# Gated cross-attention and FFN on one core: statements of the head and of the tail put in another order

## The reference, cut to what matters

```python
def xattn(query, ctx, mask, Wq, bq, Wk, bk, Wo, bo):        # one head of 256
    Q, K = query @ Wq.T + bq, ctx @ Wk.T + bk
    scores = where(mask[:, None, None, :], -inf, Q K^T)      # 16 batches, 128 x 128 each
    return softmax(scores) @ ctx @ Wo.T + bo                 # V is ctx itself

def ffn(x, weights, scale, bias):
    w = (weights >= 0) * 2 - 1
    return clip((x @ w.T) * scale + bias, -100, 100)

x = x + tanh(g_xattn) * xattn(layernorm(x), ctx, ...)        # x, ctx: 16 x 128 x 256, fp32
x = x + tanh(g_ffn) * ffn(layernorm(x), ...)
```

## Time and profile before

| what | value |
|---|---|
| median of 3 runs | 76.68 us (76.57 to 77.14) |
| the profiled execution's own time | 76.77 us |
| its span (first to last instruction) | 74.9 us |
| TensorE (PE) busy | 68.6 us, 92% |
| VectorE (DVE) busy | 57.9 us, 77% |
| GpSimd (POOL) busy | 53.7 us, 72% |
| ScalarE (ACT) busy | 42.9 us, 57% |
| mean granted TensorE clock | 0.993 |

### The profile page before, as it was taken

The page is one execution under the profiler, slowest core; times in us unless marked ns, Lnnn a source line. Parts: engine busy times, 40 slices in busy tenths (PEclk is TensorE's granted clock), DMA queues, the critical chain, the costliest instruction groups (busy, mean ns, idle before and its releaser), DMA issues.

```text
span 74.9 us, 1593 instructions
## 1 busy us (share of the span) xinstructions
PE 68.6 (92%) x509; PEld 64.2 (86%) x509; DVE 57.9 (77%) x186; ACT 42.9 (57%) x116; POOL 53.7 (72%) x107
## 2 busy tenths in 40 slices
PE   4999988999999999999999999999999999988700
PEld 4988777999999999999999999999999999844400
DVE  0082996975965778999899989999959895949780
ACT  1501528489989639963977495669548607453000
POOL 4000327988989989497999899989899589984700
PEclk9999999999999999999999999999999999999997
DMA  0898999999970000004000300210040000080133
GB/s 6 278 264 214 289 280 244 257 347 371 346 235 30 4 4 4 9 0 140 0 0 27 113 0 9 94 47 0 0 140 1 0 0 0 13 276 4 65 103 113
DMA packets 8229, 8.10 MB, mean 108 GB/s; under 512 B 537, under 2 KB 8093, under 8 KB 8221
## 3 DMA queue, kind: packets, MB, share of 16 engines
q1 hardware_dynamic: 8212, 8.00, 35.1%
q10 hardware_dynamic: 8, 0.00, 0.0%
HBM read 5.90 MB, written 2.10 MB: 107 GB/s over the span
## 4 chain that ended last, share of the span: by engine, by line
PE 75%; DVE 9%; ACT 4%; issue 4%; POOL 3%; POOLq 1%; ACTq 0%
PE ps_K L630 15%; PE ps_Z L630 13%; PE ps_S L630 10%; PE ps_xT L625 8%; PE ps_O L708 8%; PE ps_F L630 8%; PE ps_F L758 6%; PE ps_cT L625 3%; PE ps_S L700 2%; POOL y_biased L371 2%; POOL y_clip L344 1%; DVE y_biased L490 1%; POOLq L41 1%; ACT K_sb L212 1%; DVE out_sb L501 1%
## 5 line engine op out<-in xcount | busy, mean ns | idle before, releaser
L371 POOL TENSOR_TENSOR y_biased<-y_scaled,bias_g 128x256 f32<-128x256 f32 x14 | 11.7, 859 | 2.4 <-DVE y_scaled L510 2.0
L367 POOL TENSOR_TENSOR xb_sb<-x_sb,bo_g 128x256 f32<-128x256 f32 x16 | 11.4, 737 | 0.0
L222 ACT ACTIVATE p_sb<-t_sb,smin 128x128 f32<-128x128 f32 x16 | 6.4, 401 | 8.0 <-DVE smin L453 8.0
L630 PE MATMUL ps_Z<-woT_hi,cT_hi 128*128 128x256 f32 x32 | 9.7, 303 | 0.0
L212 ACT ACTIVATE K_sb<-ps_K,u_col 128x256 f32<-128x256 f32 x14 | 5.9, 474 | 6.5 <-PE ps_K L630 6.5
L630 PE MATMUL ps_K<-cT_hi,wqk_hi 128*128 128x256 f32 x30 | 8.8, 295 | 0.3 <-DVE cT_lo L440 0.3
L630 PE MATMUL ps_Z<-woT_hi,cT_lo 128*128 128x256 f32 x32 | 9.0, 283 | 0.0
L630 PE MATMUL ps_Z<-woT_lo,cT_hi 128*128 128x256 f32 x32 | 9.0, 282 | 0.0
L630 PEld LDWEIGHTS ps_S<-K_sb,xT 128*128 128x128 f32 x64 | 8.2, 191 | 0.8 <-issue 0.4
L630 PE MATMUL ps_S<-K_sb,xT 128*128 128x128 f32 x64 | 8.6, 277 | 0.2 <-ACT K_sb L248 0.2
L630 PE MATMUL ps_K<-cT_lo,wqk_hi 128*128 128x256 f32 x30 | 8.5, 283 | 0.0
(11 more groups left out here) (130 smaller groups left out, 199.7 us busy)
## 6 DMA issues: line engine op xcount, KB each, us to landing
x_sb<-in_x_dram SPq DMA_DIRECT2D x8, 256.0 KB, 7.9
ctx_sb<-in_ctx_dram SPq DMA_DIRECT2D x8, 256.0 KB, 7.7
out_dram<-out_sb SPq DMA_DIRECT2D x7, 256.0 KB, 2.1
wq_sb<-in_L_xattn_Wq_dram SPq DMA_DIRECT2D x1, 256.0 KB, 3.0
wk_sb<-in_L_xattn_Wk_dram SPq DMA_DIRECT2D x1, 256.0 KB, 3.2
wo_sb<-in_L_xattn_Wo_dram SPq DMA_DIRECT2D x1, 256.0 KB, 5.5
mask_u<-in_mask_BxS_bk_dram SPq DMA_DIRECT2D x1, 256.0 KB, 6.2
w_sb<-in_L_ffn_weights_dram SPq DMA_DIRECT2D x1, 256.0 KB, 7.5
```

What stands on the lines that cost most here:

```text
L222: nc.scalar.activation(p_sb[:, g % 2, b], t_sb[:, g % 2, b], ACT.Exp, scale=-1.0, bias=smin[:, r:r + 1], accum_out=psum_p[:, r:r + 1]).the ...
L367: nc.gpsimd.tensor_tensor(xb_sb[:, r], x_sb[:, r], bo_g[:], ALU.add).then_inc(xb_done, 1)
L371: nc.gpsimd.tensor_tensor(y_biased[:, g % 2, b], y_scaled[:, g % 2, b], bias_g[:, 0], ALU.add).then_inc(biased_done, 1)
L630: last = nc.tensor.matmul(dst, lhsT, rhs, start=(n == 0), stop=(n == len(pairs) - 1))
```

## The change

Head: on VectorE `stats_x(0)` and the addition of eps move in front of the first weight split, and the normalising of group 0 in front of the second; `stats_x(1)` goes behind the copy of the transposed x of group 0, `stats_x(2)` behind `split_cT(1)`; `w_mid` moves from ScalarE to VectorE; `stats_x(3)` goes from in front of the loop into round 1, behind `scale_y(0)`. On GpSimd `norm_of_x(3)` goes into round 1, behind `rstd_of_x1(0)` and in front of `add_bo(1)`. On ScalarE `normalise_x(2)` goes behind `evict_K(1)`, and `exp(1, 0)` in front of `evict_xT(2)`. On TensorE `transpose_x(0)` goes in front of `project_first_K(0)`, whose six products now wait one by one for their operands; `scores(0)` becomes `first_scores`, whose first half needs only the first half of K; in round 1 `scores(1)` goes in front of `transpose_x(2)`.

Tail: `add_x1(4)` on VectorE goes behind the row minima, the scaling of group 6 and the last reciprocals. The add of group 6 is split: first batch on GpSimd, second on VectorE, behind `last_y(0)`. Clip and add of the last group's first batch go to GpSimd, behind the two `rstd_of_last_x1`. GpSimd's `clip(6)` waits for `add_x1(4)`, whose buffer it writes. The stores' waits follow.

```diff
@@ sync
-                if g == L - 2:
-                    sp.wait_ge(pool_out_done, GB)
+                if g < L - 2:
+                    sp.wait_ge(out_done, g + 1)
                 else:
-                    sp.wait_ge(out_done, g + 1 if g < L - 2 else g)
+                    sp.wait_ge(pool_out_done, GB + g - L + 2)
+                    if g == L - 1:
+                        sp.wait_ge(out_done, L - 1)
...
@@ scalar
-            normalise_x(2)
             for i in range(1, L):
                 evict_K(i)
                 if i == 1:
-                    act.wait_ge(w_mean_ready, 1)
...
-                evict_xT(i + 1)
-                exp(i, 0)
+                    normalise_x(2)
+                    exp(1, 0)
+                    evict_xT(2)
+                else:
+                    evict_xT(i + 1)
+                    exp(i, 0)
                 evict_x1T_hi(i - 1)
                 exp(i, 1)
@@ gpsimd
             mask_terms(1)
-            norm_of_x(3)
             fold_affine()
...
                 if i == 1:
                     rstd_of_x1(0)
+                    norm_of_x(3)
                     add_bo(1)
...
             add_bias(L - 1)
+            pool.wait_ge(out_done, L - 2)
             clip(L - 1)
+            add_x1_of(L - 1, 0)
             for b in range(GB):
                 rstd_of_last_x1(b)
+            pool.wait_ge(last_biased_done, 1)
+            nc.gpsimd.tensor_scalar(y_clip[:, L % 2, 0], y_biased[:, L % 2, 0], lim[:, 0:1], lim[:, 1:2],
+                                    ALU.min, ALU.max).then_inc(pool_clip_done, 1)
+            add_x1_of(L, 0)
@@ vector
+            stats_x(0)
...
             dve.wait_ge(wqk_hi_ready, 1)
             nc.vector.tensor_tensor(wqk_lo[:, 0], ...)
-            stats_x(0)
...
+            dve.wait_ge(rstd_first_done, 1)
+            ...xn[:, b] of group 0...
             dve.wait_ge(wqk_hi_ready, DC)
             nc.vector.tensor_tensor(wqk_lo[:, 1], ...)
             split_cT(0)
...
-            stats_x(1)
             dve.wait_ge(xT_prod, 1)
             nc.vector.tensor_scalar(xT[:, 0], ps_xT, 1.0, None, ALU.add).then_inc(xT_done, 1)
+            stats_x(1)
...
-            stats_x(2)
             mask_and_min(0)
             split_cT(1)
+            stats_x(2)
...
-            stats_x(3)
+            dve.wait_ge(w_mean_ready, 1)
+            for c in range(DC):
+                nc.vector.tensor_scalar(w_mid[:, c], w_sign2[:, c], w_mean[:, c:c + 1], None, ALU.add).then_inc(w_mid_ready, 1)
             for i in range(1, L):
...
                 scale_y(i - 1)
                 if 2 <= i < L - 1:
                     add_x1(i - 2)
+                if i == 1:
+                    stats_x(3)
                 if i + 3 < G:
                     stats_x(i + 3)
...
-            add_x1(L - 3)
             mask_and_min(L)
...
                 nc.vector.reciprocal(recip_p[:, r:r + 1], psum_p[:, r:r + 1]).then_inc(recip_done, 1)
+            add_x1(L - 3)
...
+            last_y(0)
             dve.wait_ge(pool_clip_done, 2 * GB)
-            nc.vector.tensor_tensor(out_sb[:, rows(L - 1)], y_clip[:, (L - 1) % 2], x1_sb[:, rows(L - 1)], ALU.add
+            nc.vector.tensor_tensor(out_sb[:, L * GB - 1], y_clip[:, (L - 1) % 2, 1], x1_sb[:, L * GB - 1], ALU.add
                                     ).then_inc(out_done, 1)
-            last_y(0)
-            clip_last(0)
             last_y(1)
-            add_last_x1(0)
-            clip_last(1)
-            add_last_x1(1)
+            clip_last_y()                      # clip and add of the second batch
@@ tensor
+            transpose_x(0)
             project_first_K(0)
-            transpose_x(0)
...
-            scores(0)
+            first_scores()                     # chunk c = 0 of both batches waits for K_done 1, c = 1 for K_done 2
...
                 if i == 1:
                     attend(0)
+                    scores(1)
                     transpose_x(2)
+                    transpose_ctx(2)
+                    transpose_x1(0)
+                    pe.wait_ge(w_mid_ready, DC)
+                    transposes(ps_wT, w_mid).then_inc(ps_wT_ready, 1)
                 else:
                     transpose_x(i + 1)
                     attend(i - 1)
-                scores(i)
...
```

More of the change, by code:

```diff
@@ L177, in _ @@
             for g in range(L):
-                if g == L - 2:
-                    sp.wait_ge(pool_out_done, GB)
-                else:
-                    sp.wait_ge(out_done, g + 1 if g < L - 2 else g)
+                if g < L - 2:
+                    sp.wait_ge(out_done, g + 1)
+                else:
+                    sp.wait_ge(pool_out_done, GB + g - L + 2)
+                    if g == L - 1:
+                        sp.wait_ge(out_done, L - 1)
                 sp.dma_start(out_rows[:, rows(g), :], out_sb[:, rows(g), :]).then_inc(stored, 16)
-            for b in range(GB):
-                sp.wait_ge(out_done, L - 1 + b + 1)
-                sp.dma_start(out_rows[:, L * GB + b, :], out_sb[:, L * GB + b, :]).then_inc(stored, 16)
+            sp.wait_ge(pool_out_done, GB + 2)
+            sp.dma_start(out_rows[:, L * GB, :], out_sb[:, L * GB, :]).then_inc(stored, 16)
+            sp.wait_ge(out_done, L)
+            sp.dma_start(out_rows[:, L * GB + 1, :], out_sb[:, L * GB + 1, :]).then_inc(stored, 16)
             sp.wait_ge(stored, 16 * (G + 1))
@@ L345, in clip, with add_x1_of @@
                                             ALU.min, ALU.max).then_inc(pool_clip_done, 1)
+            def add_x1_of(g, b):
+                pool.wait_ge(pool_clip_done, GB * (g - L + 2) + b + 1)
+                nc.gpsimd.tensor_tensor(out_sb[:, GB * g + b], y_clip[:, g % 2, b], x1_sb[:, GB * g + b], ALU.add
+                                        ).then_inc(pool_out_done, 1)
             def add_x1(g):
                 for b in range(GB):
-                    pool.wait_ge(pool_clip_done, b + 1)
-                    nc.gpsimd.tensor_tensor(out_sb[:, GB * g + b], y_clip[:, g % 2, b], x1_sb[:, GB * g + b], ALU.add
-                                            ).then_inc(pool_out_done, 1)
+                    add_x1_of(g, b)
             def scale_weights(c):
@@ L491, in last_y, with clip_last_y @@
                                                in1=bias_g[:, 0], op0=ALU.mult, op1=ALU.add).then_inc(last_biased_done, 1)
-            def clip_last(b):
-                dve.wait_ge(last_biased_done, b + 1)
-                nc.vector.tensor_scalar(y_clip[:, L % 2, b], y_biased[:, L % 2, b], lim[:, 0:1], lim[:, 1:2],
+            def clip_last_y():
+                r = B - 1
+                dve.wait_ge(last_biased_done, GB)
+                nc.vector.tensor_scalar(y_clip[:, L % 2, 1], y_biased[:, L % 2, 1], lim[:, 0:1], lim[:, 1:2],
                                         ALU.min, ALU.max).then_inc(clip_done, 1)
[L498 to L501, removed]
+                dve.wait_ge(clip_done, L - 1)
+                nc.vector.tensor_tensor(out_sb[:, r], y_clip[:, L % 2, 1], x1_sb[:, r], ALU.add).then_inc(out_done, 1)
             def scale_y(g):
@@ L538, in _ @@
                                         ).then_inc(wq_neg_ready, 1)
+            stats_x(0)
+            dve.wait_ge(mv_x_done, GB)
+            nc.vector.tensor_scalar(ve_x[:, rows(0)], mv_x[:, rows(0), 1], EPS, None, ALU.add).then_inc(ve_first_done, 1)
             dve.wait_ge(wqk_hi_ready, 1)
@@ L541, in _ @@
                                     ).then_inc(wqk_lo_ready, 1)
-            stats_x(0)
-            dve.wait_ge(mv_x_done, GB)
-            nc.vector.tensor_scalar(ve_x[:, rows(0)], mv_x[:, rows(0), 1], EPS, None, ALU.add).then_inc(ve_first_done, 1)
+            dve.wait_ge(rstd_first_done, 1)
+            for b in range(GB):
+                nc.vector.tensor_scalar(xn[:, b], x_sb[:, b], mv_x[:, b, 0:1], rstd_x[:, b:b + 1], ALU.subtract, ALU.mult
+                                        ).then_inc(xn_first_done, 1)
             dve.wait_ge(wqk_hi_ready, DC)
@@ L662, in project_first_K @@
             def project_first_K(m):
-                pe.wait_ge(cT_lo_done, 1)
-                pe.wait_ge(wqk_lo_ready, DC)
-                accumulate(ps_K0[m], K_pairs(0, m)).then_inc(ps_K0_ready, 1)
+                w = [[t[:, c, m * P:(m + 1) * P] for c in range(DC)] for t in (wqk_hi, wqk_lo)]
+                pairs = ([(w[0][c], cT_hi[:, 0, c]) for c in range(DC)] + [(w[1][c], cT_hi[:, 0, c]) for c in range(DC)]
+                         + [(w[0][c], cT_lo[:, 0, c]) for c in range(DC)])
+                for n, (lhsT, rhs) in enumerate(pairs):
+                    if n == 0:
+                        pe.wait_ge(wqk_hi_ready, DC)
+                        pe.wait_ge(cT_hi_done, 1)
+                    elif n == DC:
+                        pe.wait_ge(wqk_lo_ready, DC)
+                    elif n == 2 * DC:
+                        pe.wait_ge(cT_lo_done, 1)
+                    last = nc.tensor.matmul(ps_K0[m], lhsT, rhs, start=(n == 0), stop=(n == len(pairs) - 1))
```

(14 more changed lines are left out.)

7 lines of the change are left out of this document (removed).

## The result

The changed kernel takes **82.58 us** (median of 6 runs, 82.17 to 82.91), the kernel before 76.81 beside it (6 runs, 76.57 to 77.35): **1.074 times, interval 1.069 to 1.079, slower by 5.8 us**. The profiled execution took 82.62 with a span of 80.8, against 74.9.

A forecast was written before the change was run, and what follows sets the result against it. TensorE, busy throughout the 48.80 us middle stretch, was taken as the bound. Group 3's chain 4.3, head 0.2 and tail 0.2 sum to 4.7; 76.77 + 4.7 = 81.5, as a median 81.4 us, range 79.9 to 83.2.

The forecast's parts named there:

- the likeliest case: Whole kernel: group 3's chain delays TensorE, head and tail add a little, the clock stays up; 81.4 us, chance 0.58.
- the first rival: Clock falls to the lower level in TensorE's stall in round 1, costing 1.3 us more: 82.7 us, chance 0.28.
- the waits of ScalarE and GpSimd: Sign in the profile after: ScalarE waits for GpSimd's last norm step, GpSimd for VectorE's statistics of group 3.
- the wait for the copy: Sign in round 1: TensorE waits for the copy of x of group 2, before transpose_x1(0).
- the wait before `scores(2)`: Sign behind the stall: TensorE waits before scores(2), forecast to start at 30.7 against 26.45.
- adds of 1.1 in the tail: Sign in the tail: adds of about 1.1 on both VectorE and GpSimd, 0.68 and 0.73 alone.
- Group 3's chain up to its transposes: Round 1, from scale_y(0) over VectorE, GpSimd and ScalarE: TensorE transposes group 3 at about 28.7, not 25.14, +3.5 us.
- `attend(1)`, forecast +3.7: Behind the stall: evict_PT(1), queued behind normalise_x(3), is late, so attend(1) starts at 29.3 against 25.58.
- The step to `scores(2)`: Behind attend(1): scores(2) waits for the copy of group 3's transposed x, +4.3 us in all, bounds 4.0 to 4.6.
- The clock, forecast at nothing in the likeliest case: Around the stall: three stretches of TensorE work speak against a fall; as a rival priced at 1.3, bounds 0.3 and 3.5.
- The head, forecast +0.2: Head to round 1: TensorE's lead of about 0.85 is lost at residual(0) and transpose_x1(0); +0.2, between -0.4 and +0.5.
- The tail, forecast +0.2 within -0.5 to +0.4: Tail: last x1 may come earlier, but VectorE and GpSimd adding at once take longer; +0.2 us.

The follow-up runs named there:

- e3: Changed kernel with fourteen products of zeros on TensorE between K of group 2 and transpose_x(3): 81.05 us, ratio 1.0556 to the kernel before.
- e1: Changed kernel with group 3's statistics and factors back in front of the loop, head and tail still changed: 77.02 us, ratio 1.0009 to the kernel before.
- e2: Kernel before with only group 3's two statements, stats_x(3) and norm_of_x(3), moved into round 1: 82.19 us, ratio 1.0728.
- e4: Changed kernel with only VectorE's stats_x(3) back in front of the loop, norm_of_x(3) left in round 1: 77.11 us, ratio 1.0036 to the kernel before.
- e5: Kernel before with the whole tail of the change and nothing else: 76.66 us, ratio 0.9991.
- e8: Changed kernel with group 3 undone, group 2's statistics and factors earlier, round 1's old order, and of the tail only group 4's add moved: 76.19 us, 0.9935 of before.

## Why the prediction was right, and where it was not

The sign, the place and the range were right; the likeliest case was not. It had the clock stay up, at 81.4. What came was the first rival, the clock falling in the stall, at 82.7 against 82.58, to which I had given half the chance of the forecast. By the sign that the prediction set itself, a granted clock at half for several us, its likeliest case was wrong: it was so for 3.4 us. Of the other signs the stall, the waits of ScalarE and GpSimd and the wait for the copy came; the wait before `scores(2)` and adds of 1.1 in the tail (0.90 and 0.73) did not. The terms, with the span's 5.9 as the sum (FFN of group 0 ends at 24.46 against 23.87, the end of the head's share):

- **Group 3's chain up to its transposes, forecast +3.5: held.** 29.21 less 25.14 is 4.07; 3.48 of it is beyond the head's 0.59. The steps came in the order told, VectorE, GpSimd's four steps, ScalarE, TensorE, each within 0.1 of its forecast place when the head's 0.59 is taken off. The steps between the instructions of the chain, put at 0.05 to 0.15 each without a row, took 0.02 to 0.14. `attend(1)`, forecast +3.7: in e3 4.40 less its head of 0.66 (24.25 + 0.28 against 23.87), 3.74.
- **The step to `scores(2)`, "+4.3 in all": failed.** I put these scores behind the copy of group 3's transposed x. They need group 2's x and K, and e3 shows them starting with hardly a wait behind `attend(1)`: 4.48 less 0.66, **3.8**. By the medians, e3 less e1, it is 4.0, the lower bound that I gave. I had read one copy too many off ScalarE's queue: what an instruction waits for is its own semaphore, not whatever stands last in the queue that feeds it.
- **The clock, forecast at nothing in the likeliest case: the step that failed.** The argument was the end of the trace, some 3 us without a product before the clock was down, against a stall of 3.4, and three stretches of work around the waits. Those stretches did not hold it up. In after the clock came down behind the stall, in e2 inside it, and both paid. The stall was as long as the idle stretch whose end I had read, which should have made this the likeliest case. As a rival it was priced at 1.3; it costs 1.5 (e3). One row behind that price was misread: over the kernel's first products the profile shows a granted clock of 1.00, so they do not show the lower level, though they take 0.24 each and those of e3 0.12. The Trainium skill (TensorE: Matmul & The Clock Gate, Part 1) has an idle array go to half clock and sustained work bring it back. The traces of after and e2 agree in that.
- **The head, forecast +0.2: mechanism right, +0.59 in the profiled execution.** Both named waits came, `residual(0)` for `add_bo(0)` and `transpose_x1(0)` for the copy. But `norm_of_x(2)` started at 15.41, not 15.15, and x of group 0 had landed 0.3 later than in the earlier trace rows. The landing differs from run to run by more than the term (3.3 to 4.7), so that a forecast of this part to 0.2 was finer than one trace allows. Over ten runs each, e1 and e4, which keep head and tail, are slower than before by 0.1 and 0.3 by their ratios, so +0.2 is not refuted and 0.59 is not what the head costs on average.
- **The tail, forecast +0.2 within -0.5 to +0.4: 0.0**, as e5 has it too (0.9991). The gain at the last x1 was there in full (0.30 of 0.31), and so were the stretched instructions; what I left out is that the last pair of `rstd` came out at 1.09 instead of 1.45, with no add of VectorE at its start. The Trainium skill (SBUF — State Buffer, section "SBUF: two separate sides") lets a VectorE instruction with two SBUF inputs, or in a two-port mode, and a GpSimd instruction shut each other out for a whole instruction. `ve` ends 0.03 and the clip 0.16 behind GpSimd's add, while `y_biased`, with an input from PSUM, keeps its 0.47 to 0.48 beside GpSimd's clip: so far the trace agrees. The clip is held although its row starts 0.07 ahead of the add's, and the rule's price, my +0.4, was too high for the whole.

3.8 + 1.5 + 0.6 + 0.0 = 5.9, the span's difference: the forecast case with a smaller chain, and the clock rival on top of it. By medians the parts are 4.0 for the chain, 1.5 for the clock and 0.2 for head and tail together, each uncertain by 0.3 to 0.6. That the rival's 82.7 came within 0.2 of the time owes something to errors of opposite sign, and is luck to that extent: a chain too long by 0.5 and a tail by 0.2, a head too short by 0.4 and a clock by 0.2.

## What to carry to other kernels

Statistics that need only an early load belong in front of the loop, or at least ahead of any instruction on that engine that waits for another: placed behind `scale_y(0)`, 1 us of VectorE's work became a chain over four engines and 3.3 us of idle TensorE. Where a trace shows the clock come down behind an idle TensorE, a stall of like length in the middle of the work is to be priced at the lower clock from the start; products of zeros bring that part back (1.5 us here), the right order brings back all. Work given to GpSimd beside VectorE's adds and clips stretched instructions of VectorE (0.66 for 0.17, 0.95 for 0.41): of the tail's edits only the one that filled VectorE's own wait showed a gain (0.3 us). A lead won for TensorE in the head lasts only if the engines that feed it can follow: in e8 0.65 us of it shrank to 0.13 within two rounds.

## What the runs showed of the hardware

- The fall of the clock is not tied to the stall's length alone: with the same 3.30 us of stall it came in e2 at 28.0, with TensorE still standing, and in after at about 29.6, with it at work again. It differs between executions of one kernel too: the other two of e2 have a mean clock of 0.979 instead of 0.958 and take 1.1 us less, and the slowest of after's six (82.91) has 0.964 instead of 0.979. TensorE was busy throughout when it came back, at 33.0 in after and at about 34.8 in e2.
- Products of zeros, 0.12 apart, hold the clock at 1.00 through 3.3 us (e3).
- An instruction of VectorE on two numbers per partition can take 0.66 instead of 0.17 when GpSimd adds beside it (L624 against L609), and `w_mid` took 1.21 in e8 beside GpSimd's `add_bo(0)`, in after 0.62 for the same pair.
